# Attention and mixture of experts on one core: transposed probabilities by VectorE squares and SBUF transfers in place of TensorE transposes

## The reference

```
x = x + gamma * attention(layernorm(x), ctx, ctx)
    # per head: qk = q^T k / sqrt(128); sm = softmax(qk); ret[d, q] = sum_l sm[q, l] * v[d, l]
n = layernorm(x)
hid = relu(n @ W1 + b1);  alpha = softmax(hid @ W2 + b2)
x = x + sum_k alpha_k * (n @ V_k^T) @ U_k^T
```

## Time and profile before

| | us |
|---|---|
| median of 3 runs (1776.59 to 1777.09) | 1776.61 |
| span of the profiled execution | 1775.2 |
| TensorE busy | 1739.8 (98%) |
| VectorE busy | 1137.6 (64%) |
| ScalarE busy | 774.0 (44%) |
| GpSimd busy | 473.1 (27%) |
| bytes moved | 159.98 MB, 90 GB/s over the span |

### The profile page before, as it was taken

One profiled execution on the slowest core, in us unless ns is written; L12 is line 12 of the kernel. 1 busy time (PEld: TensorE's weight loads), 2 busy tenths in 40 slices (PEclk: granted clock), 3 DMA queues, 4 the chain that ended last, 5 costly groups with the idle time before them and its releaser, 6 DMA issues.

```text
span 1775.2 us, 25213 instructions
## 1 busy us (share of the span) xinstructions
PE 1739.8 (98%) x8736; PEld 1394.5 (79%) x8736; DVE 1137.6 (64%) x1608; ACT 774.0 (44%) x1314; POOL 473.1 (27%) x297
## 2 busy tenths in 40 slices
PE   7999999999999999999999999999999999999999
PEld 5778787878787877878787778787877878787877
DVE  7888888898888888888889743232423333232312
ACT  5666666666666666666666431212122121212120
POOL 4444445353544444444534200000000000000000
PEclk9999999999999999999999999999999999999999
DMA  4632323332334333333333403121121203021202
GB/s 149 220 102 95 113 86 110 93 118 95 118 95 118 95 112 101 95 115 88 109 93 106 160 1 107 36 95 47 65 77 37 105 0 138 4 101 40 95 0 72
DMA packets 73389, 159.98 MB, mean 90 GB/s; under 512 B 17552, under 2 KB 17552, under 8 KB 73360
## 3 DMA queue, kind: packets, MB, share of 16 engines
q1 hardware_dynamic: 73360, 159.59, 28.1%
HBM read 125.87 MB, written 33.69 MB: 90 GB/s over the span
## 4 chain that ended last, share of the span: by engine, by line
PE 85%; DVE 11%; issue 2%; ACT 1%; DMA 0%; DVEq 0%; POOL 0%
PE scores L850 20%; PE attended L429 16%; PE scores L396 15%; PE scores L893 10%; PE turned L410 10%; PE turned L911 5%; PE attended L911 5%; DVE q L507 4%; DVE pt_lo L486 3%; PE scores L930 2%; DVE neg_max L477 2%; DVE scaled L527 2%; ACT pt_hi L343 1%; PE turned L865 1%; PE turned L868 1%
## 5 line engine op out<-in xcount | busy, mean ns | idle before, releaser
L343 ACT ACTIVATE pt_hi<-turned 128x512 fp32r<-128x512 f32 x512 | 304.7, 595 | 314.9 <-PE turned L410 314.9
L410 PE MATMUL turned<-ident,probs 128*128 128x128 f32 x2048 | 388.9, 272 | 3.3 <-ACT probs L348 2.6
L410 PEld LDWEIGHTS turned<-ident,probs 128*128 128x128 f32 x2048 | 282.7, 140 | 100.8 <-ACT probs L348 19.4
L477 DVE TENSOR_REDUCE neg_max<-scores 128x1 f32<-128x1024 f32 x256 | 312.2, 1219 | 72.5 <-PE scores L396 67.6
L486 DVE TENSOR_TENSOR pt_lo<-turned,pt_hi 128x512 fp32r<-128x512 f32 x512 | 328.9, 683 | 30.9 <-ACT pt_hi L343 20.3
L348 ACT ACTIVATE probs<-scores,neg_max 128x1024 f32<-128x1024 f32 x256 | 285.9, 1117 | 48.0 <-DVE neg_max L477 47.9
L429 PE MATMUL attended<-pt_hi,v_hi 128*128 128x512 f32 x512 | 243.9, 476 | 18.8 <-DVE scaled L527 18.8
L429 PE MATMUL attended<-pt_hi,v_lo 128*128 128x512 f32 x512 | 223.6, 437 | 0.0
L429 PE MATMUL attended<-pt_lo,v_hi 128*128 128x512 f32 x512 | 223.2, 436 | 0.0
L988 DVE TENSOR_TENSOR ht_lo<-hidden,ht_hi 128x512 fp32r<-128x512 f32 x64 | 44.3, 693 | 258.6 <-ACT ht_hi L797 258.6
L850 PE MATMUL scores<-nt_hi,w_hi 128*128 128x512 f32 x512 | 200.0, 391 | 0.0
(11 more groups left out here) (102 smaller groups left out, 2805.0 us busy)
## 6 DMA issues: line engine op xcount, KB each, us to landing
x_raw<-in_x SPq DMA_DIRECT2D x32, 512.0 KB, 4.1
k_raw<-in_ctx SPq DMA_DIRECT2D x32, 512.0 KB, 3.3
v_raw<-in_ctx_t SPq DMA_DIRECT2D x32, 512.0 KB, 5.6
x_res<-in_x SPq DMA_DIRECT2D x32, 512.0 KB, 5.4
gain_row<-gains SPq DMA_DIRECT2D x64, 256.0 KB, 4.7
x<-x_out SPq DMA_DIRECT2D x64, 256.0 KB, 5.0
first_n<-x SPq DMA_DIRECT2D x32, 512.0 KB, 3.3
result<-x SPq DMA_DIRECT2D x64, 256.0 KB, 3.9
```

The lines of the kernel that those rows point to most:

```text
L343: nc.scalar.activation(pt_hi[half][:, 4 * part:4 * part + 4, col:col + P], src[:], ACT.Copy).then_inc(s_hi, 1)
L410: ins = pe.transpose(dst[:, i % 4, :], probs[j % 2][:, i * P:(i + 1) * P], ident[:])
L477: nc.vector.tensor_reduce(neg_max[:, j:j + 1], scores[j % 2][:], AX_X, ALU.max, negate=True).then_inc(s_max, 1)
```

## The change

TensorE turns no probabilities any more. VectorE transposes `probs` in squares of 32x32 (`blocks`, one instruction for 128x1024) into `pb`, with the 32 columns of each square beside those of the other steps, so that four steps make runs of 128 elements (512 bytes). When four steps are done, 16 transfers from SBUF to SBUF bring the squares to the right partitions, `pt`: each takes 32 partitions by 8 key blocks by 128 elements. Eight of them are started by SP, eight by ScalarE (`gather` in `sync` and in `scalar`). For five of the eight key blocks (`SPLIT = 5`) ScalarE makes hi and GpSimd lo, in quarters of one, one, one and two key blocks, and TensorE the three `float32r` products; for the other three one product of plain float32 operands, `v_nat` by `pt`, is made. The values' products stand ten steps behind the scores (`LAG = 10`), ScalarE's copy eight, GpSimd's subtraction nine. `attended` has two banks.

Work moves, too. ScalarE takes over the hi parts of keys and values, the normalised queries and the gains; GpSimd keeps the lo parts and gets those of the probabilities. The weights W1 and V lie where `pb` and part of `pt_hi` are now, and are loaded only at the end of the attention; the split of the first W1 columns goes from GpSimd to ScalarE and VectorE, after the attention's last work. Loads of x and of the residual move in SP's order.

```diff
@@ vector
-        def low_probs(t, j, part):
-            s_hi, s_lo = (s_hi0, s_lo0) if part == 0 else (s_hi1, s_lo1)
...
-            nc.vector.tensor_tensor(pt_lo[half][at], src[:], as_f32(pt_hi[half][at]),
-                                    ALU.subtract).then_inc(s_lo, 1)
+        def blocks(t, j, h):
+
+            half = j // HALF
+            dve.wait_ge(s_exp, t + 1)
+            if j % HALF == 0 and not (isinstance(h, int) and h == 0):
+                dve.wait_ge(s_gather[half], h * GATHERS)
+            nc.vector.transpose(pb[half][:, :, j % HALF, :], probs[j % 2][:]).then_inc(s_blocks, 1)
@@ scalar
+        def high_probs(quarter):
...
+            count, half, q, head, parity = quarter
+            if q == 0:
+                act.wait_ge(s_gather[half], head * GATHERS + GATHERS)
+            if not (isinstance(head, int) and head < 1):
+                act.wait_ge(s_pv, count - (JB - 1))
+            nc.scalar.activation(hi[half][q][:], pt[2 * parity + half][:, slice(*QUARTER_KEYS[q]), :],
+                                 ACT.Copy).then_inc(s_pthi, 1)
+
+        def gather(h, n, half, parity):
+
+            act.wait_ge(s_blocks, n + 4 * half + 4)
+            dst = pt[2 * parity + half]
+            for a in range(QB // 2, QB):
+                for g in range(QB):
+                    act.dma_start(dst[SB * g:SB * g + SB, :, P * a:P * a + P],
+                                  pb[half][SB * a:SB * a + SB, g::QB, :, :].rearrange("p k j c -> p k (j c)")
+                                  ).then_inc(s_gather[half], 16)
...
+                high_probs(quarter_in(h, n, j, parity, LAG - 2))
+                if j == 0 and not last:
+                    high_keys(h + 1, n + JB, 1 - parity)
+                if j == 2:
+                    high_values(h, n, parity)
+                if j == 1 and not first:
+                    gather(h - 1, n - JB, 1, 1 - parity)
+                if j == 5:
+                    gather(h, n, 0, parity)
                 if j == 5 and not last:
+                    queries(h + 1, 1 - parity)
                     high_queries(h + 1, n + JB, 1 - parity)
@@ gpsimd
+        def low_probs(quarter):
...
+            pool.wait_ge(s_pthi, count + 1)
+            nc.gpsimd.tensor_tensor(pt_lo[2 * parity + half][:, keys, :], pt[2 * parity + half][:, keys, :],
+                                    as_f32(hi[half][q][:]), ALU.subtract).then_inc(s_ptlo, 1)
@@ sync, slot
+            gather(h, n, 0, parity)
             if more:
-                sp.wait_ge(s_ksplit, h * 2 + 4)
-                load_k(h + 2)
                 sp.wait_ge(s_q32, h + 2)
                 load_x(h + 2)
@@ sync, end
+        gather(h - 1, n - JB, 1, 1)
+        sp.wait_ge(s_gather[0], heads * GATHERS)
+        for tile, dram in shared["w1_low_loads"]:
+            sp.dma_start(tile, dram).then_inc(shared["s_w1_low"], 16)
...
+        sp.wait_ge(s_gather[1], heads * GATHERS)
+        for k, (tile, dram) in enumerate(shared["w1_high_loads"]):
+            sp.dma_start(tile, dram).then_inc(shared["s_w1_high"][k], 16)
@@ scalar and vector, mixture
+        act.wait_ge(shared["s_pv"], KB * (tiles - 1))
+        split_weights(0)
...
+        split_weights(0)
```

More of the change, by code:

```diff
@@ new lines, in slot @@
+        def slot(h, n, parity, first, last):
+            early = isinstance(h, int) and h < 2
+            for j in range(JB):
+                low_probs(quarter_in(h, n, j, parity, LAG - 1))
+                if j == 1 and not last:
+                    low_keys(h + 1, 1 - parity)
+                if j == 3:
+                    low_values(h, parity)
+                    if not early:
+                        add_residual(h - 2, 1)
+                if j == 4 and not last:
+                    scale_of_queries(h + 1, 1 - parity)
+                if j == 6 and not last:
+                    low_queries(h + 1, 1 - parity)
+                if j == 7 and not first:
+                    add_residual(h - 1, 0)
+                if last and j in (4, 6):
+                    first_factor(j // 2 - 2)
@@ L346, in exps, with gather @@
+        def gather(h, n, half, parity):
+            act.wait_ge(s_blocks, n + 4 * half + 4)
+            dst = pt[2 * parity + half]
+            for a in range(QB // 2, QB):
+                for g in range(QB):
+                    act.dma_start(dst[SB * g:SB * g + SB, :, P * a:P * a + P],
+                                  pb[half][SB * a:SB * a + SB, g::QB, :, :].rearrange("p k j c -> p k (j c)")
+                                  ).then_inc(s_gather[half], 16)
         def exps(s, j, b):
             act.wait_ge(s_max, s + 1)
+            if not (isinstance(s, int) and s < 2):
+                act.wait_ge(s_blocks, s - 1)
@@ L367, in slot @@
                     high_queries(h + 1, n + JB, 1 - parity)
-        act.wait_ge(s_k_in, 16)
-        nc.scalar.activation(k_hi[0][:], k_raw[:], ACT.Copy).then_inc(s_ksplit, 1)
+                if last and j in (5, 7):
+                    normalise_first((j - 5) // 2)
+        high_keys(0, 0, 0)
+        queries(0, 0)
         high_queries(0, 0, 0)
         h, n = over_heads(act, slot)
-        for part in range(2):
-            high_probs(n - 1, JB - 1, n - JB, part, False)
-        for u in range(2 * FIRST):
+        gather(h - 1, n - JB, 1, 1)
@@ L376, in scalar, with first_high @@
+        gains(h - 1, 0)
+        def first_high(u):
             act.wait_ge(s_turn, u + 1)
             nc.scalar.activation(shared["nt_hi"][first_place(u)], first_turned[u % 2], ACT.Copy).then_inc(s_hi, 1)
+        for j in range(4):
+            high_probs(quarter_in(h, n, j, 0, LAG - 2))
+            first_high(j)
+        gains(h - 1, 1)
+        normalise_first(2)
+        normalise_first(3)
+        for j in range(4, JB):
+            high_probs(quarter_in(h, n, j, 0, LAG - 2))
+            first_high(j)
@@ L593, in vector @@
         variance(0, 0)
-        queries(0, 0)
         dve.wait_ge(s_qhi, 1)
```

526 lines of the change are left out of this document (269 added, 257 removed).

## The result

The changed kernel takes 1862.47 us (median of 4 runs, 1856.06 to 1868.11) against 1776.85 us: a ratio of 1.048, interval 1.0452 to 1.0507. It is slower; forecast were 1696 us and a range that ended at 1805. The profiled execution has a span of 1856.5 us.

A forecast was written before the change was run, and what follows sets the result against it. TensorE was taken to bound attention. Per head 23.4 + 1.0 old stalls + 2.5 ScalarE's burst + .6 late transfers = 27.5 us; 843.7 + 31 x 27.5 gave 1696 us, range 1603 to 1805.

The forecast's parts named there:

- ScalarE's burst: Steps 5 and 1: eight transfer starts between exponentials stall a head 2.5 us, from nothing up to 6 if the queue is full.
- a late x: Attention loop: the load of x now stands behind SP's share of the gather, costing .6 us a head.
- What bounds before: Attention before the change: TensorE bounds a head of 30.35 us, of which 64 transposes take 7.2.
- TensorE's, VectorE's, GpSimd's sums: Work per head after the change: TensorE 23.4 us, VectorE 22.6, GpSimd 22.6.
- old stalls: Attention loop: TensorE's stalls from before the change, taken as 1.0 us a head, stay.
- Rival D: VectorE's squares wait for GpSimd, 1.2 us more each: a head of 33.2 us, 1873 us, slower; chance .05.
- The rule on starters: Gather: a second starter saves only starting time, so SP alone could start all sixteen and the 2.5 us be had back.
- 26 ns a packet: Gather: middle price of a 512-byte packet, 24.6 us of transfers a head, hidden; lower end 20.5 ns, upper 46.5.
- Rival B: Gather: 32-partition transfers run at half rate, 200 GB/s; a head of 29 us, 1743 us, still faster; chance .15.
- Rival C: Gather: packets cost setup plus data; a head of 35.1 us, 1932 us; decides from 36.7 ns a packet; chance .13.
- The tail: From last scores to mixture: last gather, its split and W1's late load add 7 us to the earlier 20.4.
- the favoured case: Whole kernel: a head of 27.5 us, 1696 us, own range 1650 to 1736; chance .47.

The follow-up runs named there:

- one transfer a half: Changed kernel with the gather left out; SP starts one transfer a half copying pb to pt in 128 partitions: 1664.08 us, period 25.93.
- burst alone: Changed kernel without the gather's small packets; ScalarE still starts eight 32-packet transfers in one piece, SP one per half: 1864.61 us, period 32.04.
- SP alone: Changed kernel with all 16 starts a half on SP, x's load on ScalarE, gains before weights W1 at the end: 1869.95 us, period 32.43.
- the split in pieces: Changed kernel with ScalarE's eight starts as 3, 3, 2 over three steps, x started by ScalarE, gains before weights: 1771.72 us, period 29.70.
- the kernel with pieces and x: Changed kernel with ScalarE's eight starts as 3, 3, 2 over three steps and x's load started by ScalarE: 1790.78 us, period 29.82.

## Why the prediction was wrong

The miss in the profiled execution (1856.5 and 1.8 around it against 1696) is 162 us: 31 x (32.03 - 27.5) = 140 in the loop, 46.5 - (21.1 + 7) = 18 between scores and mixture, 2 in the mixture. The 4.5 a head in the loop are 6.1 - 2.5 = 3.6 of ScalarE's burst and .9 of the rest: 25.93 without starts and small packets, where 24.4 and .6 for a late x were taken.

- **What bounds before, TensorE's, VectorE's, GpSimd's sums: right in the main.** A square's mean is 1.24 us, starts 1.16 apart (1.15 taken); GpSimd's forms are 1.29 and 2.38 as in the earlier trace rows; a plain float32 product adds .87 (.46 from its start to the scores behind it, and these then start .87 apart instead of .46; .92 taken). With one transfer a half the head is 25.93; the sum of engines and old stalls was 24.4, so 1.5 stalls more than of old are left, of which VectorE's waits for x (13.3 us in 340) can be 1.0. Rival D fell. Two slips without weight: GpSimd's terms add up to 22.7, and 1.14 is the distance of two starts in the earlier trace rows, the reduction itself takes 1.21.
- **ScalarE's burst: the step that failed.** The place was right and the mechanism too, the size wrong: 2.5 us a head, measured 6.1 (burst alone against one transfer). Three parts of the term: the price was taken as .46 from the loads of the earlier trace rows, the nearest row, but a transfer of this shape takes .62 to .66 whatever it carries, and eight in a burst 6.3, not 3.7; step 1 was thought nearly free (.5), yet ScalarE stands there as long as in step 5 (4.8) and TensorE 1.81 us; and TensorE's low clock after the stop of 3.08 us was no term at all. How the 6.1 divide among the three was not measured. The working had named "up to 6" as its upper end and put it down to a full queue, then centred on 2.5.
- **The rule on starters** (Trainium skill, "DMA: Bandwidth & Descriptors", "Issuing engines are not separate DMA queues"). By it the split saves only the time of starting, usually small. Here that time is 10 us a half and decides: SP alone gives 32.4 us a head, the split in pieces 29.7. The split was right and only its burst wrong. The sentence that by that rule the 2.5 could be had back is refuted by that run.
- **Transfers.** The middle of 26 ns a packet holds for 128 partitions (24 to 26 by the windows), not for 32 (34). In the changed kernel this lay beneath the burst; with pieces it bounds. Rival B gave T = 29 for it, and the kernel with pieces and x has 29.8. The Trainium skill, "SBUF — State Buffer", "Door 1: The DMA port swizzle", says that 32 partitions reach half the ports; the runs agree in direction, with 238 against 339 GB/s (.70, not .5). Rival C (packets cost setup plus data) fell: 24 ns is hardly more than the 20.5 of pure rate, and even the 34 in 32 partitions stay under the 36.7 from which it decides.
- **Late x: .6 taken.** VectorE waited 5.4 us in 200 for it, about .9 a head. The size was near, but by luck, since the reason given (x behind SP's share of the gather) is not what held it. SP's row, beside ScalarE's above:

```profile
539.76 5.36 SPq L224 DMA_DIRECT2D pt<-pb  x7
546.91 0.33 SPq L201 DMA_DIRECT2D x_raw<-in_x  x1
```

  SP was through with its share at 545.12. The load waited until ScalarE had made the queries out of the old x (545.65 to 546.89), behind its own burst.
- **The tail: +7 taken, +25 measured** (46.5 against 21.1). The gains' 2 KB queue behind W1's loads: the order accounts for 4.9 of it. 41.7 us remain even with one transfer a half, so most of the rest is not the packets. That it is the last half's chain through ScalarE, GpSimd and TensorE, one after another, is argued; how it divides was not tried further.
- **The range** ended at T = 31.0, which is just the sum with 6 for the burst (23.4 + 1.0 + 6 + .6), and had no case "the same burst, but dearer", the continuation of its own largest unproven term. The burst as measured gives 27.5 + 3.6 = 31.1 or 1808 us, at the range's edge; the .9 of the rest and the tail carry it beyond. Of the slower rivals neither came: C and D fell, and the time got slower by a term of the favoured case.

## What to carry to other kernels

In these kernels a transfer's start was an instruction of the engine whose queue holds it: it was free up to the length of what the engine was running (two starts, 1.25 us, beside an exponential), and beyond that it stopped the engine (4.7 to 4.8 us in a burst of eight). So spread such starts one to three behind each long instruction, and count starts, not bytes. When a shuffle is moved to transfers, measure one transfer of exactly that shape (partitions, packet, source) for its start and its rate before taking a plain load's price. An unproven term whose upper end changes the sign of the result deserves a case of its own.

## What the runs showed of the hardware

- The start of a 32-partition SBUF-to-SBUF transfer takes .62 to .66 us as a median, with 256 packets, 128 or 32 alike, and eight in one piece on ScalarE 6.3 us in the changed kernel; a plain load of 128 partitions in the same kernel .33 to .35.
- A transfer over 128 partitions with packets of 512 bytes has the same start price (.645) but moves 339 GB/s, in 32 partitions 238 GB/s.
- After TensorE had stood 3.08 us, its clock was granted at .50 (1.2 GHz) for about 3 us and at 1.00 (2.4 GHz) again from 553 us on, and the six score products took 1.8 times as long.
- SP alone, starting such transfers one after another, kept the 16 engines at a share of .78 and 197 GB/s (all starts on SP, x on ScalarE); SP and ScalarE together 238 GB/s at 1.17.
